# Quantised and grouped attention sublayers as one program, with the ends of their pipelines interleaved

## The reference, cut to what matters

```python
def _L1_attn_ref(hidden_states, ...):      # the quantised stage, "d"
    result, ch_bias, n = _chunk_decompose(hidden_states.reshape(bsz * tgt, H))
    Q, K, V = ...   # result @ quantised W + ch_bias @ W, + bias
    probs = jax.nn.softmax(jnp.einsum('bqhd,bkhd->bhqk', Q, K), axis=-1)
    ctx = jnp.einsum('bhqk,bkhd->bqhd', probs, V).reshape(bsz * tgt, H)
    r2, cb2, n2 = _chunk_decompose(ctx)
    return r2 @ WO + cb2 @ o_weight.T + o_bias

def _L1_xattn_ref(q, k, v, ...):           # the grouped stage, "e"
    score = jnp.einsum('bhqd,bhkd->bhqk', qh, kh) / math.sqrt(HEAD_DIM)
    out = jnp.einsum('bhqk,bhkd->bqhd', jax.nn.softmax(score, axis=-1), vh)
    return out @ Wfc.T + bfc
```

## Time and profile before

| what | us |
|---|---|
| median of the runs shown | 2824.95 |
| all three runs | 2815.61, 2828.30, 2824.95 |
| the profiled execution | 2816.05 |
| its span, first to last instruction | 2814.3 |
| mean granted TensorE clock in it | 0.966 |

### The profile page before, as it was taken

The page is one execution under the profiler, slowest core; times in us unless marked ns, Lnnn a source line. Parts: engine busy times, 40 slices in busy tenths (PEclk is TensorE's granted clock), DMA queues, the critical chain, the costliest instruction groups (busy, mean ns, idle before and its releaser), DMA issues. The chain is left out here.

```text
span 2814.3 us, 66190 instructions
## 1 busy us (share of the span) xinstructions
PE 2633.4 (94%) x23860; PEld 2283.6 (81%) x23860; DVE 1902.7 (68%) x4152; ACT 1414.5 (50%) x3352; POOL 1184.3 (42%) x1559
## 2 busy tenths in 40 slices
PE   7999999996999999999999979996999999699995
PEld 7999999985888888888888868885777777477774
DVE  6655566555777777777777744443899988366676
ACT  3222222223666666666666633332666666266665
POOL 2211121123676776767767601112244344334444
PEclk9999999998999999999999989997999999799998
DMA  5000000001000000000000020000000000000001
GB/s 189 8 7 7 7 4 7 7 8 53 7 4 4 6 4 6 4 6 4 4 6 4 2 79 0 0 0 30 13 13 7 11 7 4 27 32 26 26 12 60
DMA packets 43391, 49.60 MB, mean 18 GB/s; under 512 B 3952, under 2 KB 33616, under 8 KB 43056
## 3 DMA queue, kind: packets, MB, share of 16 engines
q1 hardware_dynamic: 43312, 48.55, 5.3%
HBM read 35.96 MB, written 4.19 MB: 14 GB/s over the span
## 5 line engine op out<-in xcount | busy, mean ns | idle before, releaser
L587 POOL TENSOR_TENSOR a_probs<-a_probs,a_rs 128x512 f32<-128x512 f32 x64 | 70.6, 1102 | 468.0 <-DVE a_rs L443 468.0
L1108 ACT ACTIVATE b_probs<-bank,b_shift,b_q_scale 128x128 f32<-128x128 f32 x512 | 228.2, 461 | 0.7
L1173 POOL TENSOR_TENSOR b_rows<-b_rows,b_swapped 128x512 f32<-128x512 f32 x160 | 204.5, 1287 | 56.8 <-DVE b_swapped L946 56.8
L531 ACT COPY a_pT<-bank 128x512 f32<-128x512 f32 x64 | 37.5, 586 | 308.4 <-PE bank L324 308.4
L1220 POOL TENSOR_TENSOR b_probs<-b_probs,b_rs 128x512 f32<-128x512 f32 x128 | 133.1, 1040 | 138.5 <-DVE b_rs L998 135.2
L448 DVE TENSOR_TENSOR a_oT<-bank,a_oT 128x512 fp32r<-128x512 f32 x128 | 82.5, 686 | 142.1 <-ACT a_oT L536 142.1
L1183 POOL TENSOR_TENSOR b_rms<-b_rms,sh_minus_half 128x8 f32<-128x8 f32 (+1 forms) x128 | 170.4, 1331 | 10.6
L954 DVE TENSOR_REDUCE b_ss<-b_squares 128x4 f32<-128x512 f32 x192 | 125.2, 680 | 73.4 <-ACT b_squares L1083 73.4
L46 PE MATMUL bank<-a_xT,early_wq 128*128 128x256 f32 x512 | 149.9, 293 | 13.1 <-DVE early_wq L73 10.3
L46 PE MATMUL bank<-early_wo,b_oT 128*128 128x256 f32 x512 | 150.4, 294 | 1.4 <-DVE b_oT L920 1.4
L46 PE MATMUL bank<-early_wo,a_oT 128*128 128x256 f32 x512 | 145.3, 284 | 4.0 <-DVE a_oT L448 4.0
(11 more groups left out here) (385 smaller groups left out, 9053.1 us busy)
## 6 DMA issues: line engine op xcount, KB each, us to landing
a_xT_in<-in_xT SPq DMA_DIRECT2D x16, 256.0 KB, 2.6
sh_x<-in_x SPq DMA_DIRECT2D x1, 4096.0 KB, 18.3
b_ctx_in<-in_ctxT SPq DMA_DIRECT2D x32, 128.0 KB, 2.0
d_x_in<-sh_x SPq DMA_DIRECT2D x16, 256.0 KB, 2.3
e_x_in<-sh_x SPq DMA_DIRECT2D x16, 256.0 KB, 2.3
e_cT<-in_ctxT SPq DMA_DIRECT2D x32, 128.0 KB, 2.5
out<-sh_x SPq DMA_DIRECT2D x16, 256.0 KB, 2.1
a_qT<-in_L_attn_Wq SPq DMA_DIRECT2D x4, 512.0 KB, 6.0
```

Source lines behind the costliest of these rows:

```text
L1108: op = act.activation(probs[:, g % 2, keys], bS[:, keys], ACT.Exp, bias=shift[:, g % 2, a:a + 1], scale=q_scale[:, g, a // 2, a % 2:a % 2 ...
L1173: pool.tensor_tensor(rows[:, unit, :], rows[:, unit, :], swapped[:, half, :], ALU.add).then_inc(added[unit], 1)
```

## The change

The two blocks become one, `quantised_and_grouped_block`. `four_deep` gets a first and a last turn, and can leave out part of its fill and drain. The quantised stage runs turns 0 to 15 with `drain=0`, the grouped stage runs as turns 16 to 31 with `fill=3` (`fill=2` on DVE), and between them each engine has a written-out list, `from_first_to_second`, with the steps of the quantised stage's last three turns and of the grouped stage's first three mixed. The grouped stage's steps are those of before under names with `g_`; they use the quantised stage's semaphores, `x_in`, `keys`, `kT`, `qT`, `probs`, `pT` and `att`. Semaphores that only the grouped stage counts are set forward by the 16 turns. SP waits for the first stage's `norm_done` before it loads the rows of turns 0, 1, 2 and, once, for that of turn 15 before turn 3. The fills of the grouped `v` move to the start. Nothing is computed that was not computed before.

```diff
@@ -1694,432 +1694,17 @@
     return nth(i.n, 1, 0)
 
 
-def four_deep(engine, n_turns, turn):
+def four_deep(engine, first, before, turn, fill=0, drain=3):
 
     def of(n):
-        return Turn(n, n % 2) if 0 <= n < n_turns else None
-    for n in range(4):
+        return Turn(n, n % 2) if first <= n < before else None
+    for n in range(first + fill, first + 4):
         turn(of(n), of(n - 1), of(n - 2), of(n - 3))
-    with engine.Fori(2, n_turns // 2) as j:
+    with engine.Fori(first // 2 + 2, before // 2) as j:
         for k in range(2):
             turn(Turn(j * 2 + k, k), Turn(j * 2 + (k - 1), 1 - k), Turn(j * 2 + (k - 2), k), Turn(j * 2 + (k - 3), 1 - k))
-    for n in range(n_turns, n_turns + 3):
+    for n in range(before, before + drain):
         turn(of(n), of(n - 1), of(n - 2), of(n - 3))
...
 
-def quantised_attention_block(nc, sh):
+def quantised_and_grouped_block(nc, sh):
 
 
...
+        g_xT = g_sb("xT", [128, C, 256])
+        g_cT = g_sb("cT", [128, C, 256])
+        g_v = g_sb("v", [128, 2, 4, 8, VW])
+        g_attT = g_sb("attT", [128, C, 256])
+        g_xb = g_sb("xb", [128, 2, D])
+        g_c_loaded = nc.alloc_semaphore("e_c_loaded")
+        g_x_taken, g_k_taken, g_att_taken = g_sem("x_taken"), g_sem("k_taken"), g_sem("att_taken")
+        g_xb_ready, g_res_ready = g_sem("xb_ready"), g_sem("res_ready")
         n_turns = sh.turns // 2
+        d13, d14, d15, e0, e1, e2 = (Turn(n, n % 2) for n in range(n_turns - 3, n_turns + 3))
         block = ctx.enter_context(nc.Block())
 
...
+            for s in g_looped:
+                sp.sem_inc(s, 1 + n_turns)
+            sp.sem_inc(g_c_loaded, 1)
+            for r in range(2):
+                sp.dma_start(g_cT[:, :, r * 128:(r + 1) * 128], t["ctxT"][r]).then_inc(g_c_loaded, 16)
+            sp.wait_ge(norm_done, nth(0, 1, 1))
+            sp.wait_ge(qx.turned, this(d15))
+            sp.dma_start(x_in[:, :, :], sh.x[:, 0:2, :]).then_inc(x_loaded, 16)
+
+            def load_next(i):
+                sp.wait_ge(qx.turned, nth(i + (n_turns - 1), 1, 1))
+                sp.dma_start(x_in[:, :, :], sh.x[:, bass.ds(i * 2, 2), :]).then_inc(x_loaded, 16)
+                sp.wait_ge(v_ready, nth(i + (n_turns - 1), 1, 1))
+                for r in range(2):
+                    sp.dma_start(g_cT[:, :, r * 128:(r + 1) * 128],
+                                 t["ctxT"][bass.ds(i * 2 + r, 1)].rearrange("a p c n -> (a p) c n")).then_inc(g_c_loaded, 16)
+            for n in range(1, 3):
+                sp.wait_ge(norm_done, nth(n, 1, 1))
+                load_next(n)
+            sp.wait_ge(norm_done, this(d15))
+            with sp.Fori(3, n_turns) as i:
+                load_next(i)
...
+            def g_turn_x(i, oldest):
+                if i is None:
+                    return
+                pe.wait_ge(x_loaded, nth(i.n, 1, 1, 16))
+                if oldest is not None:
+                    pe.wait_ge(g_att_taken, this(oldest))
+                else:
+                    pe.wait_ge(g_k_taken, last(i))
+                for r in range(2):
+                    for c in range(C):
+                        op = pe.transpose(bX[0][:, c * 256 + r * 128:c * 256 + (r + 1) * 128], x_in[:, r, c * 128:(c + 1) * 128], sh.ident[:, :])
+                op.then_inc(qx.turned, 1)
...
+            def from_first_to_second():
+                project_out(d13, 1)
+                turn_att(d14)
+                turn_probs(d15, 0)
+                scores(d15, 2, 1)
+                turn_probs(d15, 1)
+                pe.wait_ge(scaled, this(d13))
+                g_turn_x(e0, None)
+                scores(d15, 3, 3)
+                turn_probs(d15, 2)
+                weigh(d15, 1)
+                weigh(d15, 0)
+                turn_probs(d15, 3)
+                g_project_k(e0)
+                turn_probs(d15, 4)
+                weigh(d15, 2)
+                pe.wait_ge(g_k_taken, this(e0))
+                turn_cmax_att(d14)
+                turn_probs(d15, 5)
+                pe.wait_ge(qc.centred_ready, this(d14))
+                g_project_q(e0, None)
+                spread_top(d14, qc, bX[0], qc.y_scaled)
+                turn_probs(d15, 6)
+                weigh(d15, 3)
+                g_project_v(e0)
+                turn_probs(d15, 7)
+                weigh(d15, 5)
+                g_scores(e0, 0, 5, True)
+                weigh(d15, 6)
+                weigh(d15, 7)
+                project_out(d14, 0)
+                project_out(d14, 1)
+                weigh(d15, 4)
+                g_turn_probs(e0, 0, 7, True)
+                pe.wait_ge(scaled, this(d14))
+                g_turn_x(e1, None)
+                pe.wait_ge(v_taken[0], this(e0))
+                turn_att(d15)
+                g_weigh(e0, 0)
+                g_project_k(e1)
+                g_turn_probs(e0, 1, 0, False)
+                g_scores(e0, 1, 3, False)
+                g_turn_probs(e0, 2, 1, False)
+                pe.wait_ge(g_k_taken, this(e1))
+                turn_cmax_att(d15)
+                g_turn_probs(e0, 3, 2, False)
+                g_weigh(e0, 2)
+                g_weigh(e0, 1)
+                pe.wait_ge(qc.centred_ready, this(d15))
+                g_project_q(e1, None)
+                spread_top(d15, qc, bX[0], qc.y_scaled)
+                g_turn_probs(e0, 4, 3, False)
+                g_weigh(e0, 3)
+                g_project_v(e1)
+                g_turn_probs(e0, 5, 4, False)
+                g_weigh(e0, 4)
+                g_scores(e1, 0, 6, True)
+                project_out(d15, 0)
+                project_out(d15, 1)
+                g_turn_probs(e0, 6, 5, False)
+                g_weigh(e0, 5)
+                pe.wait_ge(scaled, this(d15))
+                g_turn_x(e2, None)
+                g_weigh(e0, 6)
+                g_turn_probs(e0, 7, 6, False)
+                g_project_q(e2, None)
+                g_project_k(e2)
+
+            four_deep(pe, 0, n_turns, turn, drain=0)
+            pe.wait_ge(g_w_loaded, 16 * sh.grouped.N_LOADS)
+            pe.wait_ge(zeroed, 10)
+            from_first_to_second()
+            four_deep(pe, n_turns, 2 * n_turns, g_turn, fill=3)
...
+            def from_first_to_second():
+                lowest(d14, qc, bX[1])
+                maximum(d15, 5)
+                maximum(d15, 4)
+                shift(d15, 4)
+                moments(d13)
+                widest(d14, qc)
+                maximum(d15, 6)
+                shift(d15, 6)
+                maximum(d15, 7)
+                shift(d15, 7)
+                shift(d15, 5)
+                centre(d14, qc, bX[1])
+                find_top(d14, qc, bX[0])
+                unit(d14, qc)
+                invert_unit(d14, qc)
+                thresholds(d14, qc)
+                exceed(d14, qc)
+                take_att(d15, 0, 3)
+                count(d14, qc)
+                clip(d14, qc)
+                rescale(d14, qc)
+                invert(d14, qc)
+                divide(d14, qc)
+                restore(d14, qc, y_ready)
+                g_maximum(e0, 0)
+                g_maximum(e0, 1)
+                g_shift(e0, 0)
+                g_maximum(e0, 3)
+                g_maximum(e0, 2)
+                take_att(d15, 1, 4)
+                g_shift(e0, 2)
+                g_shift(e0, 1)
+                highest(d15, qc, bX[1])
+                lowest(d15, qc, bX[1])
+                g_shift(e0, 3)
+                moments(d14)
+                widest(d15, qc)
+                centre(d15, qc, bX[1])
+                g_maximum(e0, 5)
+                g_maximum(e0, 4)
+                find_top(d15, qc, bX[0])
+                g_shift(e0, 4)
+                unit(d15, qc)
+                g_shift(e0, 5)
+                invert_unit(d15, qc)
+                g_maximum(e0, 7)
+                g_maximum(e0, 6)
+                g_shift(e0, 7)
+                g_shift(e0, 6)
+                thresholds(d15, qc)
+                exceed(d15, qc)
+                g_take_att(e0, 0, 3)
+                count(d15, qc)
+                clip(d15, qc)
+                rescale(d15, qc)
+                invert(d15, qc)
+                divide(d15, qc)
+                restore(d15, qc, y_ready)
+                g_maximum(e1, 3)
+                g_maximum(e1, 0)
+                g_maximum(e1, 1)
+                g_maximum(e1, 2)
+                g_shift(e1, 0)
+                g_shift(e1, 2)
+                moments(d15)
+                g_shift(e1, 3)
+                g_shift(e1, 1)
+                dve.wait_ge(norm_done, this(d15))
+
+            four_deep(dve, 0, n_turns, turn, drain=0)
+            from_first_to_second()
+            four_deep(dve, n_turns, 2 * n_turns, g_turn, fill=2)
...
+            def from_first_to_second():
+                g_take_x(e0)
+                exponent(d15, 4)
+                take_pT(d15, 3)
+                exponent(d15, 6)
+                g_take_k(e0)
+                take_pT(d15, 4)
+                exponent(d15, 5)
```

(99 more changed lines are left out.)

657 lines of the change are left out of this document (287 added, 370 removed).

## The result

| | kernel before | changed kernel |
|---|---|---|
| median, runs interleaved on one chip | 2820.28 us (4 runs) | 2782.43 us (4 runs, 2776.08 to 2796.25) |
| the profiled execution | 2816.05 us | 2796.25 us |
| its span | 2814.3 us | 2794.5 us |
| mean granted TensorE clock in it | 0.966 | 0.965 |

The ratio is 0.9869, with a 95% interval of 0.9838 to 0.9899: 38 us saved where 31 were forecast. The measured 2782 lies inside the range, near its lower end. The two profiled executions differ by 20 us only; why it is 20 there and 38 between the medians is taken up with the first experiment.

The account below looks back on a forecast made before the run. The seam between quantised and grouped stages, 89.05 us, was to become as long as PE's work: 51 + 3.5 (clock) + 3.5 (chain waits) = 58 us, 31 saved. Against the 2824.95 median: 2794 us, range 2779 to 2810.

Parts of the forecast that it names:

- What bounds the seam: Stretch from the quantised stage's bare drain to the first full grouped turn, 89.05 us before: priced by PE's work.
- PE's work, 48.9 us, times 1.04: In the seam: start-to-start prices at the upper clock sum to 48.9 us; small waits add 4%, giving 51 us.
- Clock, one patch at 3.5 us: In the seam: narrow work brings one patch, 7 us at half speed, 3.5 us lost; bounds none and two.
- The two chains, 3.5 us of waits: Quantiser chains of the last two quantised tiles, in the seam: PE waits 3.5 us, between 0 and 14.
- The walk: Both quantiser chains followed step by step: PE reaches the output projections at 22.7 and 44 us, just never waiting.
- Rival A: Seam bound by its chains, both as slow as in the loop: stretch 72 us, time 2808; chance 0.14.
- The gap of 4.22 us, and the loads: Between the programs: program change and first-input wait removed, inside the 89.05; first grouped input loads a turn earlier.
- The moved queues: Steps moved on POOL, SP and DVE, and POOL's fills: cost nothing; queue cover 2 to 6 us, fills hidden.
- B: Lower clock stays for the whole seam: 51 us becomes 87, time 2823, no change; chance 0.07 together with D.
- C: Loop turns of both stages grow through shared semaphores and buffers: slower, 2842 at 4 us a turn; chance 0.03.
- D: One wait in the order holds PE until a chain ends: 80 us or more, 2816; chance 0.07 with B.
- The floor of the window: Sign for the changed kernel: PE's window from the bare drain's first step to the grouped loop is 52 to 67 us.

Follow-up runs that it names:

- the first experiment: Changed kernel and kernel before, both rerun without edit: changed 2783.68 us (ratio 0.9858), later 2778.83 (0.9834); before 2815.72 in its one profiled run.
- the fills early or late: Late: changed kernel with POOL's three grouped v fills moved back to the seam, 2782.8 then 2778.94 us. Early: the changed kernel itself, 2778.83 beside the latter.
- The padded versions: Changed kernel with two or six extra 128x512 DVE operations ahead of the last quantised tile's restore: 2794.36 and 2800.27 us, one run each.
- The two coarse orders: One program against the kernel before: full drain then full fill, 2819.85 us (0.9995); whole drain and fill turns alternating, 2823.25 us (1.0004).

## Why the prediction was right

- **What bounds the seam.** Right. The stretch is PE's work: 51.30 of 51.63 us, and 48.35 of 48.69 in the profile without a patch.
- **PE's work, 48.9 us, times 1.04.** The count by starts was 48.9 us, and the stretch without a patch took 48.7. The 4% on top was the mis-sized term: it was taken from the gap between such a sum and the grouped turn's 19.24 us, and in the new order it is nothing. 2 us too much.
- **Clock, one patch at 3.5 us.** One patch fell in the first profile and cost 51.63 - 48.68 = 3.0 us. Two further profiles of the same kernel had none. The right term was nought or one by chance, so 1 to 2 us on the mean instead of 3.5, an estimate from the five profiles with the fills early or late, of which two have a patch. By the rule of the Trainium skill (TensorE: Matmul & The Clock Gate, "What's actually happening") that I weighed there, there would be no patch. In the first profile PE was busy for 7.11 of 7.11 us at 0.54, so the trace disagrees with it here too, as the earlier trace rows did; but the profiles with 1.00 fit it. Neither the rule nor my "narrow work brings it" tells which execution gets one.
- **The two chains, 3.5 us of waits.** The walk was right and the addition wrong: 0.23 us in all. The chains took 20.6 us (2386.99 to 2407.64) and 15.8 us (2412.40 to 2428.21), the walk had 20.4 and 17.2. PE came to the two output projections 23.3 and 43.2 us after the left mark, the walk had 22.7 and 44. Part of that nearness is luck, since the first profile holds a patch: in the last one, without a patch, the chains took 18.5 and 15.8 us and PE came at 20.4 and 40.2. Rival A, whose price was both chains at the loop's 26.4 us, falls. Its price was also read wrongly: 26.4 us is when PE comes to the projection, and the restore of that tile was done 2.6 us before, at 2370.18, while PE's wait there names ACT's `d_v`:

```profile
2369.49 0.69 DVE L2602 SCALAR_TENSOR_TENSOR d_qc_result<-d_qc_whole,d_qc_clipped 128x512 fp32r<-128x512 int32 x1
```

  So even the loop's chain takes 23.8 us, and both chains at that would have cost 9 us and not 14. The padded versions show how close d15's chain was: nearly all that is added to it, PE waits for.
- **The gap of 4.22 us, and the loads.** Right as a part of the 89, and by itself worth little, as the version that only joins the programs shows.
- **The moved queues.** DVE's wait is covered, the fills are covered. SP's load had 1.5 us to spare where I said 6: I had left out its landing (2.3 us), and PE needed it at 56.7 us after the mark, not at 59.5. Its issue came at 52.9 us after the left mark, walked 53.5. Cost nothing as said, on a cover four times thinner.
- **Rivals B, C, D.** B falls with a clock of 0.94 to 1.00 in the stretch, C with the grouped turn's period (19.23 us), D with 0.23 us of waiting. The two coarse orders show what D would have been: 80 to 83 us, at no gain (2820 and 2823, where I had priced it at 2816).
- **The sum.** 58 us forecast, 48.7 to 51.8 measured. The floor of the window that I named, 52 us, was just too high. The forecast missed by 2794 - 2782 = 12 us: 6 to 9 from the stretch, and most of the rest because I set the saving of 31 us against a median of 2824.95 when the runs beside the changed kernel had 2820.28. Those 5 us are part of the spread that the lower clock's patches give, for which I had widened by 6 to 8 us.
- **What it did not say.** Some 12 of the 40 us are the same work done at the upper clock: PE's busy time in the stretch went from 60.24 to 48.35 us (51.30 with a patch) with the same instructions, and its idle time from 28.8 to 0.3. The pricing by starts at the full clock held this without naming it.

## What to carry to other kernels

Where two pipelines meet, count the bounding engine's work across drain and fill by start-to-start prices at the full clock; if each dependent chain, walked hop by hop, ends no later than that engine reaches its consumer, the seam shrinks to that sum, and in this case no allowance for waits was needed on top. Interleave finer than the hops of the longest chain: joining the programs or alternating whole turns left that chain bare and gained nothing that could be measured. Compare kernels by medians of many runs and by their time at the lower clock, since two profiles of one kernel can differ by 10 us ahead of the place that was changed.

## What was not expected of the hardware

- With PE busy 3.7 to 4.0 us of every 4, the clock falls to the lower level for some 6.8 us in about every second quantised turn: in the last profile of the changed kernel the windows of 4 us at 2104, 2108 and 2160, 2164 show it.

```profile
2104.00:2108.00 4.00, 3.70 (x28) 2.89 (x25) 3.97 (x8) 2.11 (x5) 2.93 (x6) 0.71 0.02 4
2108.00:2112.00 4.00, 4.00 (x28) 2.87 (x26) 2.84 (x5) 2.41 (x5) 1.12 (x5) 0.50 0.06 24
2160.00:2164.00 4.00, 4.00 (x17) 3.42 (x17) 3.49 (x8) 1.56 (x3) 1.38 (x3) 0.54 0.00 0
2164.00:2168.00 4.00, 4.00 (x37) 2.26 (x39) 2.93 (x5) 2.24 (x4) 1.99 (x8) 0.61 0.17 66
```

  Ahead of each of these two, PE does 64 products of 18 columns (from 2102.34 and from 2156.79 us) and then the first half of an output projection at the upper clock. Twelve wide instructions more in each turn did not take the patches away (170 us of low time for 163).
- The same code gets more or fewer of them in the quantised stage's early turns from one execution to the next (0.81, 0.76, 0.83 in one profile of the changed kernel, 0.91, 1.00, 0.83 in another), and its left mark stands at 2387 or at 2377 us with it: 10 of the 22 us over which its runs spread (2774 to 2796). The runs of the kernel before spread as much (2812 to 2833) and follow their clock in the same way, but where their patches fall its two profiles, both from the faster half of its runs, do not show.
